# Deform stage: GpSimd waits for eight of a tile's nine gathers, VectorE takes the ninth at its last batch

## The reference

```
offset  = conv3x3(x, offset_w)                 # 18 channels: (dy, dx) for each of 9 taps
patches = deform_patches(x, offset)            # for each pixel and tap: four corners, bilinear weights
y    = einsum('bckhw,ock->bohw', patches, wk)
attn = sigmoid(mean(y) + std(y))               # over the pixels of an image and channel
out  = x + y * attn
```

## Time and profile before

| | us |
|---|---|
| median of three runs | 15070.81 |
| lowest to highest | 15065.17 to 15072.31 |
| the profiled execution's own time | 15021.82 |
| its span | 15020.2 |
| GpSimd busy | 7518.3 |
| TensorE matmul busy | 8857.2 |
| VectorE busy | 6520.5 |
| ScalarE busy | 3085.6 |

### The profile page before, as it was taken

The page is one execution under the profiler, slowest core; times in us unless marked ns, Lnnn a source line. Parts: engine busy times, 40 slices in busy tenths (PEclk is TensorE's granted clock), DMA queues, the critical chain, the costliest instruction groups (busy, mean ns, idle before and its releaser), DMA issues.

```text
span 15020.2 us, 156851 instructions
## 1 busy us (share of the span) xinstructions
PE 8857.2 (59%) x51639; PEld 6070.3 (40%) x51639; DVE 6520.5 (43%) x13120; ACT 3085.6 (21%) x5214; POOL 7518.3 (50%) x7657
## 2 busy tenths in 40 slices
PE   6897888888554544545454545454454545454543
PEld 2333444448443433333343434343343434343433
DVE  5655556553334444343434343434434343434333
ACT  3433444432111111111111111111111111111111
POOL 0011222212466666666666666666666666666665
PEclk9998999989666666767676766666666657676766
DMA  3322111126333333333333333333333333333332
GB/s 95 84 82 66 52 60 56 56 99 189 96 91 109 91 108 99 101 99 101 106 96 103 98 109 91 109 91 109 99 102 102 98 103 96 104 98 109 91 94 83
DMA packets 503924, 1436.05 MB, mean 96 GB/s; under 512 B 128980, under 2 KB 234196, under 8 KB 474576
## 3 DMA queue, kind: packets, MB, share of 16 engines
q0 software_dynamic: 353344, 970.88, 22.2%
q1 hardware_dynamic: 150032, 458.00, 10.1%
HBM read 1175.46 MB, written 252.90 MB: 95 GB/s over the span
## 4 chain that ended last, share of the span: by engine, by line
POOL 29%; issue 19%; DMA 13%; DVE 8%; PE 6%; another core or an unknown queue 0%; DVEq 0%; POOLq 0%; ACT 0%; ACTq 0%; SPq 0%
POOL e_g L1786 29%; DMA e_g<-table_dram,e_index_slots 12%; DVE e_g L2050 2%; PE e_ps L1903 2%; DVE e_g L2052 2%; PE e_ps L1918 2%; PE e_ps L1930 2%; PE e_ps L1939 1%; DMA e_tmp<-x3s_dram 1%; DVE e_x3t L1963 1%; DVE e_index_slots L2024 1%; DVE e_x3t L1967 0%; DVE e_w_next L2008 0%; DVE e_st L1971 0%
## 5 line engine op out<-in xcount | busy, mean ns | idle before, releaser
L1786 POOL DMA_INDIRECT e_g<-table_dram,e_index_slots x7056 | 6823.6, 967 | 4426.0 <-issue 1893.4
L1930 PE MATMUL e_ps<-k_ident,e_g 128*128 128x128 f32 x7056 | 1719.1, 398 | 4897.7 <-DVE e_g L2052 4840.2
L1930 PEld LDWEIGHTS e_ps<-k_ident,e_g 128*128 128x128 f32 x7056 | 1153.8, 197 | 5455.4 <-DVE e_g L2052 5209.6
L1939 PE MATMUL e_ps<-e_corners,e_w_def 128*64 128x128 f32 x14112 | 2667.5, 369 | 268.6 <-issue 148.9
L2024 DVE COPY e_index_slots<-e_index_now 128x9 uint32<-128x9 uint32 (+1 forms) x784 | 137.9, 177 | 5866.8 <-DMA e_g<-table_dram,e_index_slots 4314.5
L1939 PEld LDWEIGHTS e_ps<-e_corners,e_w_def 128*64 128x64 f32 x14112 | 2430.1, 197 | 463.7 <-issue 319.0
L1855 ACT ACTIVATE e_corners<-e_ps 128x512 f32<-128x512 f32 (+1 forms) x2352 | 1064.7, 489 | 4603.2 <-PE e_ps L1930 3895.9
L2049 DVE TENSOR_TENSOR e_ps<-e_g,e_ps 128x512 f32<-128x512 f32 (+1 forms) x2352 | 1324.5, 563 | 115.6 <-DMA e_g<-table_dram,e_index_slots 61.1
L2052 DVE TENSOR_TENSOR e_g<-e_g,e_ps 128x512 f32<-128x512 f32 (+1 forms) x2352 | 1301.5, 553 | 81.3
L2050 DVE TENSOR_TENSOR e_g<-e_g,e_ps 128x512 f32<-128x512 f32 (+1 forms) x2352 | 1284.8, 546 | 0.0
L1860 ACT ACTIVATE e_big<-e_ps 64x128 f32<-64x128 f32 (+1 forms) x784 | 211.8, 270 | 3518.7 <-remote 2210.0
(11 more groups left out here) (438 smaller groups left out, 8075.1 us busy)
## 6 DMA issues: line engine op xcount, KB each, us to landing
e_g<-table_dram,e_index_slots POOLq DMA_INDIRECT x7056
table_dram<-e_rt SPq DMA_DIRECT2D x32, 1624.0 KB
a_xt<-x_in SPq DMA_DIRECT2D x16, 1568.0 KB
v_dram<-a_vout SPq DMA_DIRECT2D x32, 784.0 KB, 8.5
b_xt<-v_dram SPq DMA_DIRECT2D x16, 1568.0 KB
v_dram<-b_vout SPq DMA_DIRECT2D x32, 784.0 KB, 7.5
c_v2t<-v_dram SPq DMA_DIRECT2D x16, 1568.0 KB
c_xt<-x_in SPq DMA_DIRECT2D x16, 1568.0 KB, 6.6
```

The lines of the kernel that those rows point to most:

```text
L1786: pool.indirect_dma_start(out=g[:, slot, tap * CORNERS:(tap + 1) * CORNERS], out_offset=None, in_=table, in_offset=bass.IndirectOffsetOnAx ...
L1930: mm = pe.transpose(ps[:, TURN[tap // 4], (tap % 4) * P:(tap % 4 + 1) * P], g[:, slot, tap * CORNERS:tap * CORNERS + 2 * C], k.ident[:, :])
L1939: mm = pe.matmul(ps[0:C, OUT, 0:P], w_d[:, tap, :], corners[:, tap, :], start=(tap == 0), stop=(tap == TAPS - 1))
```

## The change

The ninth gather of each slot gets a semaphore of its own, `last_gathered[slot]`. GpSimd's wait before a tile is for the preceding tile's first eight gathers only. VectorE starts a tile when eight have landed, and waits for the ninth before its third batch; the copy of the index list moves from the start of the tile to there.

```
-        gathered = [s.sem(f"gathered{n}") for n in range(SLOTS)]
+        gathered, last_gathered = ([s.sem(f"{name}{n}") for n in range(SLOTS)] for name in ("gathered", "last_gathered"))
...
-                        ).then_inc(gathered[slot], 16)
+                        ).then_inc((gathered if tap < TAPS - 1 else last_gathered)[slot], 16)
...
-                        pool.wait_ge(gathered[slot - 1], 16 * TAPS)
+                        pool.wait_ge(gathered[slot - 1], 16 * (TAPS - 1))
...
-                        pool.wait_ge(gathered[(slot - 1) % SLOTS], r * (16 * TAPS) + (16 * TAPS if slot else 0))
+                        pool.wait_ge(gathered[(slot - 1) % SLOTS], r * (16 * (TAPS - 1)) + (16 * (TAPS - 1) if slot else 0))
...
-                        dve.wait_ge(gathered[slot], r * (16 * TAPS) + 16 * TAPS)
-                        if not last:
-                            issue(slot, group * GK + (GK + slot * TAPS))
+                        dve.wait_ge(gathered[slot], r * (16 * (TAPS - 1)) + 16 * (TAPS - 1))
...
                         for n, (lo, hi) in enumerate(BATCHES):
...
+                            if hi == TAPS:
+                                dve.wait_ge(last_gathered[slot], r * 16 + 16)
+                                if not last:
+                                    issue(slot, group * GK + (GK + slot * TAPS))
```

## The result

The changed kernel is slower: 15951.05 us (15864.16 to 15977.91, four runs) beside 15067.99 (15054.44 to 15072.31) for the kernel before, a ratio of 1.0578 with a 95% interval of 1.0534 to 1.0622. The profiled execution took 15977.91 us.

What follows compares the result with a forecast made beforehand. GpSimd's gathers and its wait for the ninth landing were taken as the bound; 783 gaps by 1.25 us plus 1.25 at the end, 980 us, off 15070.8 gave 14091 us, range 13980 to 14210.

Steps and rivals of the forecast that it cites:

- The wait: GpSimd between tiles: the wait ends 1.25 us earlier, gap from ninth to next first gather 2.44 us, tile 12.44 us.
- VectorE: VectorE's start at the eighth landing: waiting for the ninth before the third batch costs nothing, covered by 2.8 us of batches.
- The copy's new place: Index copy beside the next tile's third gather: taken to cost 0, at most 0.17 us a tile, 133 us.
- The gather of 3.37 us: Gather beside a long VectorE instruction, evidence for the rival that the copy holds up gathers: 14224 us, chance 0.06.
- The disturbed tiles: 64 tiles whose first gather comes late beside output transfers: 1.25 us gained each, 80 us; bounds 0 and 350 us.
- What is late next: VectorE and TensorE between groups: blocks keep their length, 8.8 us come off 52.8 of room, nothing takes over.
- room: Time from TensorE's end of a tile's transposes to its slot's next gather: 52.8 us, forecast to become 44.
- The queue is never empty: Slower rival: at each tile's start one gather is held, the tile loses 1.17 us net, 15987 us; chance 0.01.

Runs made afterwards that it cites:

- e1: Changed kernel, but GpSimd again waits for all nine gathers of the preceding tile, VectorE staying as changed: 15148.85 us, 1.008 of the kernel before.
- e3: Changed kernel with three short GpSimd memsets as pauses in each tile, behind taps 1, 3 and 5: 14881.93 us, 0.9902 of the kernel before.
- e6: Changed kernel with two GpSimd pauses in each tile, behind the third and sixth gather: 14662.57 us, 0.97 of the kernel before.
- e11: Changed kernel with one GpSimd pause per tile in even slots, two in odd slots: 14501.8 us, 0.9632 of the kernel before.
- e2: Changed kernel, but VectorE waits for all nine gathers and copies the index list first, as before: 15896.71 us, 1.0574 of the kernel before.
- e5: Changed kernel with one GpSimd pause in each tile, behind the fifth gather: 14821.43 us, 0.9788 of the kernel before.
- e8: Changed kernel with gathers of 512 bytes an entry instead of 1024: 15821.59 us, 1.0456 of the kernel before.
- e9: Changed kernel with gathers of 64 entries instead of 128: 16124.44 us, 1.0702 of the kernel before.
- e10: Changed kernel with six of nine gathers per tile replaced by GpSimd memsets of about a gather's length: 13282.98 us, 0.882 of the kernel before.
- e7: Changed kernel with all three GpSimd pauses ahead of each tile's first gather: 15211.54 us, 1.0056 of the kernel before.

## Why the prediction was wrong

**The wait: right.** The gap was forecast at 2.44 us and is 2.43; the idle time in it 1.5, and is 1.48. Gathers start 1.25 us apart, the period is 12.44.

**VectorE: right.** It was idle for 7.50 us in front of a first batch where 7.4 were forecast, and its third batch has no wait ahead of it. The timeline of VectorE in the changed kernel, at the boundary shown above and a tile later:

```profile
6314.59 0.32 DVE L2024 COPY e_index_slots<-e_index_now 128x9 uint32<-128x9 uint32 x1
6314.70 0.39 DVE L2051 TENSOR_TENSOR e_ps<-e_g,e_ps 128x128 f32<-128x128 f32 x1
...
6329.28 0.69 DVE L2051 TENSOR_TENSOR e_ps<-e_g,e_ps 128x512 f32<-128x512 f32 x1 [7.50 <-DMA e_g<-table_dram,e_index_slots]
```

**The copy's new place: right, at nothing.** The copy at 6314.59 lies within the gather that started at 6313.96, and that one took 0.95 us. The median of all gathers went from 946 to 949 ns, 3 ns by 7056 or 21 us. Of the copies, 272 start inside a gather; these gathers have 947 ns in the middle, and none is over 1100. The hold that the Trainium skill, page "SBUF — State Buffer", section "SBUF: two separate sides", describes for a copy on VectorE isn't seen for this small one. The gather of 3.37 us, which the prediction counted for it, stood beside a SCALAR_TENSOR_TENSOR, which is no copy.

**The disturbed tiles: mis-sized.** I took a gain of 1.25 us for each, 80 us. In the changed kernel the excess over the median period is 2308 us. Taking off the 88 held gathers (2040 us less their usual 88 x 1.48) leaves some 400, an estimate, beside 414 before: next to nothing gained. e1 shows that VectorE's part alone costs 123 us there (537 less 414).

**What is late next: this is the step that failed.** It said that blocks on VectorE and TensorE between groups keep their length, that 44 us of room are left, and that "Nothing takes over". The room was right for the kernel before, where the smallest is 49.7 us, and the undisturbed tiles did get 1.22 us shorter. But TensorE's blocks don't keep their length when gathers come nine in 12.44 us: the 72 matmuls of the offset convolution took 35.6 to 46.5 us instead of 27.2 to 27.7, the 100 transposes of the offsets 21.1 to 35.1 instead of 18.0 to 21.1. And TensorE no longer catches up behind such a block. The second and third store of a group came 7.25 and 9.85 us behind the one before them, in the middle; in the changed kernel 13.04 and 12.94. So the seven slots fill, the room goes to 1.0 us, and GpSimd is held at the first tile of a group, 88 times, by 1.4 to 37.5 us.

The sum: the shorter undisturbed period gave 783 x 1.22 = 955 us, and the excess over it grew from 414 to 2308 us, by 1894, nearly all of it in the held gathers. Together the gathers, from the first to the last, take 940 us longer (12059.6 beside 11119.3), and the tile (15925.5 - 3865.8 - 10.0) / 783 = 15.39 us on average. My forecast treated the engines as independent as long as the instructions stay the same. A row that could have warned me was in the trace of before, ScalarE's 2210.0 us of waits for "remote" behind products that were recorded as over. I had looked at who bounds GpSimd, and never at whether those behind it had their results when the record said so.

**The rival on the slower side named the time, not the mechanism.** "The queue is never empty" gave 15987 us, from one gather in each tile being held to 3.37 us. The gathers themselves are not lengthened (median 949 ns; 78 of 7056 are over 1.1 us, 138 before), and in e3, e6 and e11 the next tile's first gather comes as close behind the ninth (2.40 to 2.41 us) and the kernels are faster than before. The agreement with 15951 is chance.

**What is shown and what isn't.** Shown: the loss comes from GpSimd's half of the change (e1, e2); from how densely its gathers come and not from the rule of starting early (e3, e5, e6, e11); not from their bytes (e8), their number of entries (e9), or GpSimd being busy (e10); it reaches GpSimd over TensorE's late results and the slots (the room and the held gathers of each run). In this kernel the edge lies near a period of 12.8 to 12.9 us for nine gathers. That TensorE itself works late, and not only its signals, is seen outside the tiles: in both preparing steps its own starts are spread where it waits for nobody, and the stretches are longer.

Open: what a gather does that makes TensorE late. Open too is whether the mean rate counts or the longest row of gathers without a pause: the pauses of e3, e5, e6 and e11 change both, and e7 has a rest behind each nine. Why e1 and e7 have less lateness than the kernel before is not known. A run without TensorE's products at the changed rate, or with fewer and larger gathers of the same bytes, was not tried.

## What to carry to other kernels

Before speeding up an engine that feeds a chain, look at the distance between a producer's end and its consumer's start all along the chain; a consumer that waits for "remote" behind work that is recorded as over is a sign to look further: here the same rows grew until the slots were full. Measure the room too, from the end of the work to the moment its buffer is wanted, in all tiles; the bracket alone named TensorE 136 times before the change, when it held nobody. When a removed wait makes a kernel slower, first put a small delay back elsewhere in the same loop: it tells whether the order or the rate is at fault. And a rate can have a best value between the old and the new; here one and two pauses in turn, 12.93 us a tile, beat both 13.66 and 12.44.

## What the runs showed of the hardware

- Indirect DMAs issued by GpSimd every 1.25 us, nine in 12.44 us, made TensorE's results reach ScalarE up to 40.1 us after the last product's recorded start (median 5.32); at nine in 13.12 us it was at most 5.8 us (median 0.45). The products' own recorded starts and durations don't show it (0.369 us each before, 0.370 after); two long stretches of TensorE do, 27.2 to 27.7 us becoming 35.6 to 46.5, and 18.0 to 21.1 becoming 21.1 to 35.1.
- With the granted clock at its full or at its half level the lateness was much the same, 5.71 and 6.60 us.
- Halving the bytes of each (15821.59 us) or its entries (16124.44) didn't help; putting memsets in the place of six in nine (13282.98) did.
- An indirect DMA's time on GpSimd is nearly all fixed: 0.949 us for 128 entries, 0.895 for 64.
- TensorE beside dense gathers started small transposes at distances of 0.69 to 0.71 and 1.39 to 1.40 us, and the rest in a row from 3.87 us after the last gather's start.
